# Queries with a third of the keys at whole width, the other keys in token halves, and new issue orders, in a windowed attention and MLP block

## The chip, the cores and the metric

One core of one Trainium2 chip runs the whole program. The metric is the device time of one execution in microseconds (us); less is better. Engines: PE is TensorE (matmuls; PEld its weight loads), DVE VectorE, ACT ScalarE, POOL GpSimd, SP SyncE, which here only issues DMAs.

## What is computed

The input is 32 images of 96 channels, 56 × 56 pixels. Each image is cut into 8 × 8 windows of 7 × 7 tokens:

```python
xn = layernorm(xw)                                  # per token, over 96 channels
q, k, v = split(xn @ qkv_w.T + qkv_b)               # 12 heads of 8
attn = softmax(q * SCALE @ k.T + bias[head])        # 49 x 49 per window and head
out = (attn @ v) @ proj_w.T + proj_b
x1 = x + out
bn = batchnorm(depthwise_conv3x3(x1))
y = bn + gelu(bn @ w1.T + b1) @ w2.T + b2           # hidden width 384
```

## The kernel before

A chunk is one row of windows of one image: 8 windows, 392 tokens. There are 256 chunks. Each engine has one list of steps; in step `s` (loops at L427, L557, L654, L825 and L234) it works on about ten chunks at once, each at another stage, so that chunk `c` needs some eight steps from load to output. The lists are written out by hand, in the order in which each engine issues its work; semaphores join them. `wait` waits for the producer, `free` for the last reader of a PSUM bank that is to be written again.

**The stages.** `centred` (L348) subtracts the mean with an fp32 matmul from `x_sb` into bank `d_ps`; ACT squares it, `variance` (L357) averages the squares into `b_ps`, `log_variance` and `root` (L535, L542) make 1/sqrt, DVE's `input_normal` (L804) makes `xn`, ACT's `input_high` (L549) its fp16 part `xh`, POOL's `input_low` (L594) the rest `xl`. Products of fp32 accuracy are made of three fp16 ones: high × high, high × low, low × high (`halves_three`, `whole_three`).

**Queries and keys.** `queries` (L365) writes 128 columns of weights (96 of queries and 32 that nobody reads) times 392 tokens into `a_ps`, `keys` (L372) the same for keys into `b_ps`. Both do so in two halves of 64 output partitions, three pairs of matmuls each. ACT's `query_high` and `key_high` (L511, L502) make fp16 `qh` and `kh`, 96 × 392, and DVE's `query_low` and `key_low` (L767) `ql` and `kl`. SP then copies these within SBUF into `q_all` and `k_all`, whose partitions are 32 rows of terms (4 terms × 8 dimensions) under the rows of bias, and whose free side has 12 heads × 8 windows × 50. Six DMAs per chunk do that (`term`, L209; 96 rows of 800 bytes each), and `max_scores` 0 waits for all six (L307).

**Scores.** `max_scores` p (L303) and `exp_scores` p (L282), p = 0 to 3 for two windows each, are 24 matmuls of 49 × 49, two windows side by side in the two halves of the array. DVE's `maxima` (L733) reduces the first; `maxima_rows` (L324) transposes the maxima, DVE's `maxima_out` copies them, and SP writes them as a row of `q_all` (`maximum_row`, L221), for which `exp_scores` 0 waits. ACT's `exp` (L468) makes the probabilities. `values` (L379) and `values_out` make `v32`; `values_times_p` p (L332) has 12 fp32 matmuls in four quarters of the array, each recorded as two passes. ACT's `outputs` writes them out, POOL's `to_channels` (L629) moves them with four DMAs, `log_sums`, `inverses` and `normalise` divide.

**The rest.** `projection` (L391) in fp32, `image_sum`, nine taps of the convolution (POOL two and a sum, DVE seven, L757), `image_high` and `image_low` on POOL, `hidden` k (L404), `gelu` k on ACT (L519), `second` k (L418, fp32, halves), and `block_out` (L795) on DVE, one per chunk. `hidden` 0, 1, 2 use `d_ps`, `a_ps`, `b_ps`; the three `second` accumulate in `d_ps`. ACT loads its function table twice per step (L559, L573).

**The order on PE** in a step before: `exp_scores` 2, `max_scores` 3, `projection`, `hidden` 0, `maxima_rows`, `hidden` 1, 2, `exp_scores` 3, `max_scores` 0, `second` 0, 1, 2, `keys`, `max_scores` 1, `queries`, `exp_scores` 0, `centred`, `max_scores` 2, `exp_scores` 1, `values_times_p` 2, 3, `variance`, `values`, `values_times_p` 0, 1.

Of the kernel before, what the change touches and what calls it, by code (L numbers as in the profile page):

```python
# [11 lines left out]
HD = C // HEADS  # L12
# [4 lines left out]
TOK = WS * WS  # L17
# [9 lines left out]
TERMS = 4 * HD  # L27
HIGH = ((2 * TERMS, 0, TOK),)
# [5 lines left out]
STEPS = CHUNKS + 11  # L34
# [4 lines left out]
def block_program(nc, x, w_qkv, b_qkv_row, b_v, w_proj, w_proj_rows, b_proj, ln_g, ln_b, bias_q,  # L39
                  conv_w, bn_g, bn_b, bn_mean, bn_var, w1, b1, w2, b2, eye, low, half, out):  # L40
    ctx = ExitStack()
    with ctx:
# [30 lines left out]
        qh, ql, kh, kl = (sb(n, [C, 2, NW * KP], F16) for n in ("qh", "ql", "kh", "kl"))  # L73
# [107 lines left out]
        def _(sp):  # L181
# [27 lines left out]
            def term(t, n, part, done, c):  # L209
                if not real(c):  # L210
                    return
                wait(sp, done, c)
                sp.dma_start(t[n:TERMS:4, c % 4, :, :], part[:, c % 2, :]).then_inc(exp_in[c % 4], 16)

            def first_term(t, n, part, done, c):
                if real(c):
                    wait(sp, sm_done[3], c - 4)
                    wait(sp, st_done[3], c - 4)
                    term(t, n, part, done, c)
# [29 lines left out]
        def _(pe):  # L249
# [8 lines left out]
            def halves_three(o, sh, sl, mh, ml):  # L258
# [3 lines left out]
                return halves(o, sl, mh, start=False)  # L262

# [68 lines left out]
            def values_times_p(c, p):  # L332
                if not real(c):
                    return
                if p == 0:
                    wait(pe, v32_done, c)
                wait(pe, p_done[p], c)
                if p == 0:
# [9 lines left out]
            def centred(c):  # L348
# [4 lines left out]
                free(pe, (y_done, c-8), (g_done[0], c-8), (xn_done, c-1))  # L353
# [3 lines left out]
            def variance(c):  # L357
# [4 lines left out]
                free(pe, (kl_done, c-1), (g_done[2], c-8), (sum_done, c-6), (lnv_done, c-1))  # L362
                mm(b_ps[0:C, 0:CT], avg[:, 0:C], sq[:, :], start=True, stop=True).then_inc(var_done, 1)  # L363

            def queries(c):  # L365
# [3 lines left out]
                free(pe, (g_done[1], c-7), (v32_done, c-2), (ql_done, c-1))  # L369
                halves_three(a_ps[0:128, 0:CT], wq_h[:, 0:128], wq_l[:, 0:128], xh[:, c % 2, :, 0:TOK], xl[:, c % 2, :, 0:TOK]).then_inc(q_done, 1)  # L370

            def keys(c):  # L372
# [3 lines left out]
                free(pe, (g_done[2], c-7), (sum_done, c-5), (lnv_done, c), (kl_done, c-1))  # L376
# [520 lines left out]
```

## Time and profile before

| | |
|---|---|
| median of 3 runs | 3174.46 us (3173.98 to 3175.64) |
| the profiled execution | 3164.1 us, its span 3162.3 us |
| busy: PE, PEld | 3029.4 us (96%), 2105.9 us (67%) |
| busy: DVE, ACT, POOL | 2888.8 (91%), 2768.5 (88%), 1956.6 us (62%) |
| DMA | 269,922 packets, 288.31 MB, mean 91 GB/s |
| granted PE clock, mean | 0.993 |

The span runs from the first to the last instruction. A matmul's record starts when it starts; its end is modelled, so consecutive records overlap and a busy share overstates how full PE is. "Idle before" counts the time in which the engine had no record open, and names what released it; "issue" means nothing that the profile shows. SPq is SP's issuing of DMAs.

### The profile page before, as it was taken

Reading aid. Unit: us, or ns where it says so; the run is one execution under the profiler, and the core shown is the slowest. Engines: PE = TensorE matmul, PEld = TensorE weight load, DVE = VectorE, ACT = ScalarE, POOL = GpSimd, SP = SyncE. Lnnn points to the kernel's source line nnn. Section 1 sums busy time; section 2 is a strip of 40 time slices with the busy share of each in tenths; the row PEclk is TensorE's granted clock in tenths of the full one; section 3 lists DMA queues with packets and bytes.
Section 4 is the critical chain, followed back from the end, with each engine's and each line's share of the span. In section 5 each row is a group of like instructions: output and inputs, shape, how many; then the busy total and the mean of one; then the engine's idle time right before and its main releaser. Section 6 shows DMA issues by size and latency. Waiting matters only on the chain.

```text
span 3162.3 us, 199772 instructions
## 1 busy us (share of the span) xinstructions
PE 3029.4 (96%) x88076; PEld 2105.9 (67%) x88076; DVE 2888.8 (91%) x4908; ACT 2768.5 (88%) x4867; POOL 1956.6 (62%) x2574
## 2 busy tenths in 40 slices
PE   3899999999999999999999999999999999999997
PEld 2666666666766666666666666666666676666663
DVE  4799999999999999999999999999999999999996
ACT  2799999989989999998989999988989999998986
POOL 2566666666666666666666666666666666666664
PEclk9999999999999999999999999999999999999998
DMA  1233333333333333333333333333333333333331
GB/s 40 86 91 96 91 96 94 92 95 91 97 91 94 95 94 95 96 91 95 91 96 94 94 96 94 92 96 91 95 95 93 96 97 93 95 98 91 95 92 41
DMA packets 269922, 288.31 MB, mean 91 GB/s; under 512 B 55651, under 2 KB 252580, under 8 KB 269062
## 3 DMA queue, kind: packets, MB, share of 16 engines
q1 hardware_dynamic: 236294, 198.40, 22.6%
q0 software_dynamic: 32768, 77.14, 7.0%
q8 instruction: 700, 11.47, 1.5%
q14 instruction: 160, 1.31, 0.1%
HBM read 39.34 MB, written 38.54 MB: 25 GB/s over the span
## 4 chain that ended last, share of the span: by engine, by line
PE 91%; issue 3%; ACT 2%; SPq 1%; DMA 1%; DVE 1%; POOL 0%; POOLq 0%; ACTq 0%; DVEq 0%
PE d_ps L255 21%; PE st_ps L299 12%; PE o_ps L345 11%; PE sm_ps L320 10%; PE b_ps L363 7%; PE b_ps L399 6%; PE a_ps L255 4%; PE b_ps L255 4%; PE a_ps L266 3%; PE a_ps L268 3%; PE a_ps L267 3%; PE d_ps L266 1%; PE d_ps L268 1%; PE b_ps L267 1%; PE d_ps L267 1%
## 5 line engine op out<-in xcount | busy, mean ns | idle before, releaser
L764 DVE SCALAR_TENSOR_TENSOR s<-ximg,cols,s 96x392 f32<-96x392 f32 x1792 | 1137.0, 635 | 30.7 <-POOL s L627 3.2
L738 DVE TENSOR_REDUCE mx<-sm_ps 128x12 f16<-128x588 f32 x1024 | 785.0, 767 | 127.7 <-PE sm_ps L320 125.1
L474 ACT ACTIVATE p<-st_ps 128x588 f32<-128x588 f32 x1024 | 672.4, 657 | 179.2 <-PE st_ps L299 176.1
L637 POOL DMA_DIRECT2D ox<-o_sb x1024 | 582.7, 572 | 30.8 <-ACT o_sb L499 17.2
L320 PEld LDWEIGHTS sm_ps<-k_all,q_all 127*49 127x49 f16 x24576 | 460.6, 104 | 171.5 <-issue 76.0
L255 PE MATMUL d_ps<-g,w_s 128*64 128x392 f32 x3072 | 560.2, 500 | 0.0
L299 PEld LDWEIGHTS st_ps<-q_all,k_all 128*49 128x49 f16 x24576 | 435.5, 103 | 157.2 <-issue 107.8
L610 POOL TENSOR_TENSOR s<-ximg,cols 96x392 f32<-96x392 f32 x256 | 216.0, 844 | 520.5 <-DVE y L801 519.9
L299 PE MATMUL st_ps<-q_all,k_all 128*49 128x49 f16 x24576 | 516.1, 186 | 21.4 <-issue 19.3
L320 PE MATMUL sm_ps<-k_all,q_all 127*49 127x49 f16 x24576 | 508.6, 186 | 25.9 <-issue 15.6
L599 POOL TENSOR_TENSOR xl<-xn,xh 96x392 f16<-96x392 f32 x256 | 258.8, 1011 | 273.6 <-ACT xh L555 256.5
L645 POOL CAST sh<-s 96x392 f16<-96x392 f32 x256 | 199.5, 779 | 350.0 <-DVE s L764 350.0
L345 PE MATMUL o_ps<-p,v 128*32 128x49 f32 x24576 | 384.9, 209 | 15.2 <-issue 13.1
L345 PEld LDWEIGHTS o_ps<-p,v 128*32 128x32 f32 x24576 | 308.9, 110 | 48.8 <-issue 18.8
L560 ACT ACT_TABLE_LOAD x256 | 328.4, 1283 | 4.5
L574 ACT ACT_TABLE_LOAD x256 | 328.4, 1283 | 4.4
L255 PEld LDWEIGHTS d_ps<-g,w_s 128*64 128x64 f32 x3072 | 197.2, 137 | 197.0 <-ACT g L525 116.0
L791 DVE TENSOR_TENSOR v<-a_ps,half_c 128x768 f32<-128x768 f32 x256 | 245.1, 958 | 36.1 <-PE a_ps L268 16.2
L627 POOL TENSOR_TENSOR s<-s,part 96x392 f32<-96x392 f32 x256 | 261.2, 1020 | 0.1
L652 POOL TENSOR_TENSOR sl<-s,sh 96x392 f16<-96x392 f32 x256 | 239.8, 937 | 20.5
L255 PE MATMUL d_ps<-x_sb,center 96*64 96x392 f32 x1024 | 224.1, 516 | 20.9 <-DMA x_sb<-in_x 20.9
L399 PE MATMUL b_ps<-ox,wp 96*96 96x196 f32 x1024 | 233.3, 350 | 6.3 <-DVE ox L755 5.6
(122 smaller groups left out, 5959.7 us busy)
## 6 DMA issues: line engine op xcount, KB each, us to landing
ox<-o_sb POOLq DMA_DIRECT2D x1024, 73.5 KB
k_all<-kh SPq DMA_DIRECT2D x512, 75.0 KB
q_all<-qh SPq DMA_DIRECT2D x512, 75.0 KB
x_sb<-in_x SPq DMA_DIRECT2D x256, 147.0 KB, 2.4
out<-y SPq DMA_DIRECT2D x256, 147.0 KB, 2.7
q_all<-ql SPq DMA_DIRECT2D x256, 75.0 KB
k_all<-kl SPq DMA_DIRECT2D x256, 75.0 KB
q_all<-mxt SPq DMA_DIRECT2D x256, 9.4 KB, 2.1
```

Source lines behind the costliest of these rows:

```text
L255: last = mm(o[64 * h:64 * h + 64], w[:, 64 * h:64 * h + 64], m, start=start, stop=stop)
L299: last = mm(st_ps[64 * w:64 * w + TOK, h // HH, c0:c0 + TOK], k_all[:, r, h, n:n + TOK], q_all[:, r, h, n:n + TOK], start=True, stop=True)
L320: last = mm(sm_ps[64 * w:64 * w + TOK, h // HH, c0:c0 + TOK], q_all[0:MAXROW, r, h, n:n + TOK], k_all[0:MAXROW, r, h, n:n + TOK], start=Tr ...
L345: last = mm(o_ps[32 * c4:32 * c4 + 32, at:at + TOK], v32[:, c % 2, h, p, :], p32[:, p, h, :], start=True, stop=True)
L399: last = mm(o, wp[:, 0:C], ox[:, c % 2, w, :].rearrange("c (n r k) -> c n r k", n=NP, k=WS), start=True, stop=True)
L474: af(p32[:, p, :, :].rearrange("p (b h) n -> p b h n", b=2), st_ps[:, :, 0:HALF].rearrange("p b (h n) -> p b h n", n=TOK), ACT.Exp).then_i ...
L560: act.preload_act_table_set("natural_log_exp_and_others")
L574: act.preload_act_table_set("gelu_and_others")
L627: tt(acc, acc, image(part[:, :]), ALU.add).then_inc(tap_done[1], 1)
L637: nc.gpsimd.dma_start(ox[:, c % 2, x4, :], o_sb[x4::4, c % 2, :, :]).then_inc(o_in[c % 2], 16)
L738: v.tensor_reduce(mx[:, c % 2, 0:HEADS, p].rearrange("p (b h) -> p b h", b=2), sm_ps[:, :, 0:HALF].rearrange("p b (h n) -> p b h n", n=TOK ...
L764: v.scalar_tensor_tensor(acc, image_rows(c, k // 3, k % 3), cw_c[:, k:k + 1], acc, ALU.mult, ALU.add)\
```

## The change

- `queries` writes its 96 rows and 32 rows of keys (four heads of each dimension, `K_WITH_Q`) at whole width, in three matmuls. `keys` makes the other 64 rows, into the same bank `a_ps`, for windows 0 to 3 in partitions 0 to 63 and windows 4 to 7 in partitions 64 to 127, in three pairs of 196 columns. `kh` and `kl` are now 128 × 196. The host orders the key columns to suit.
- The copies into `q_all` and `k_all` are twelve DMAs per chunk: three of queries (96 rows of 800 bytes), three of the third of the keys (32 rows of 800 bytes), six of the rest (64 rows of 400 bytes).
- The banks of `hidden` 0, 1, 2 become `a_ps`, `b_ps`, `d_ps`; `second` accumulates in `b_ps`, in the order 0, 2, 1.
- All five lists have a new order, with some work in the next or the previous step; there is one more step.

```diff
-STEPS = CHUNKS + 11
+K_WITH_Q = 4
+ARRIVALS = 12
+STEPS = CHUNKS + 12
-        qh, ql, kh, kl = (sb(n, [C, 2, NW * KP], F16) for n in ("qh", "ql", "kh", "kl"))
+        qh, ql = (sb(n, [128, 2, NW * KP], F16) for n in ("qh", "ql"))
+        kh, kl = (sb(n, [128, 2, NP * KP], F16) for n in ("kh", "kl"))
...
+            def third_of_keys(n, part, done, c):
...
+                wait(sp, done, c)
+                sp.dma_start(k_all[n:TERMS:4, c % 4, 0:K_WITH_Q, :], part[C:128, c % 2, :]).then_inc(exp_in[c % 4], 16)
+
+            def rest_of_keys(n, part, done, c):
...
+                wait(sp, done, c)
+                for i in range(2):
+                    sp.dma_start(k_all[n:TERMS:4, c % 4, K_WITH_Q:, i * NP * KP:(i + 1) * NP * KP],
+                                 part[64 * i:64 * i + 64, c % 2, :]).then_inc(exp_in[c % 4], 16)
...
             for s in range(STEPS):
+                store(s - 12)
                 load(s)
-                first_term(k_all, 0, kh, kh_done, s - 3)
-                term(k_all, 2, kh, kh_done, s - 3)
-                term(q_all, 0, qh, qh_done, s - 3)
-                term(q_all, 2, ql, ql_done, s - 3)
-                term(k_all, 1, kl, kl_done, s - 3)
-                term(q_all, 1, qh, qh_done, s - 3)
-                store(s - 11)
-                maximum_row(s - 4)
+                maximum_row(s - 5)
+                claim_terms(s - 3)
+                query_term(0, qh, qh_done, s - 3)
+                third_of_keys(2, qh, qh_done, s - 3)
+                third_of_keys(1, ql, ql_done, s - 3)
+                query_term(1, qh, qh_done, s - 3)
+                third_of_keys(0, qh, qh_done, s - 3)
+                query_term(2, ql, ql_done, s - 3)
+                rest_of_keys(0, kh, kh_done, s - 3)
+                rest_of_keys(2, kh, kh_done, s - 3)
+                rest_of_keys(1, kl, kl_done, s - 3)
...
+            def token_halves_three(o, sh, sl, mh, ml):
+
+                terms = ((sh, mh), (sh, ml), (sl, mh))
+                for i, (s, m) in enumerate(terms):
+                    for h in range(2):
+                        last = mm(o[64 * h:64 * h + 64], s, m[:, NP * h:NP * h + NP], start=i == 0, stop=i == 2)
+                return last
...
-                    wait_ring(pe, exp_in, c, 6 * 16)
+                    wait_ring(pe, exp_in, c, ARRIVALS * 16)
...
             def queries(c):
                 if not real(c):
                     return
                 wait(pe, xl_done, c)
-                free(pe, (g_done[1], c-7), (v32_done, c-2), (ql_done, c-1))
-                halves_three(a_ps[0:128, 0:CT], wq_h[:, 0:128], wq_l[:, 0:128], xh[:, c % 2, :, 0:TOK], xl[:, c % 2, :, 0:TOK]).then_inc(q_done, 1)
+                free(pe, (g_done[0], c-7), (v32_done, c-2), (kl_done, c-1), (ql_done, c-1))
+                whole_three(a_ps[:, 0:CT], wq_h[:, 0:128], wq_l[:, 0:128], xh[:, c % 2, :, 0:TOK], xl[:, c % 2, :, 0:TOK]).then_inc(q_done, 1)
 
             def keys(c):
                 if not real(c):
                     return
                 wait(pe, xl_done, c)
-                free(pe, (g_done[2], c-7), (sum_done, c-5), (lnv_done, c), (kl_done, c-1))
-                halves_three(b_ps[0:128, 0:CT], wq_h[:, 96:224], wq_l[:, 96:224], xh[:, c % 2, :, 0:TOK], xl[:, c % 2, :, 0:TOK]).then_inc(k_done, 1)
+                free(pe, (ql_done, c), (g_done[0], c-7), (v32_done, c-2), (kl_done, c-1))
+                token_halves_three(a_ps[:, 0:NP * TOK], wq_h[:, 128:192], wq_l[:, 128:192], xh[:, c % 2, :, 0:TOK], xl[:, c % 2, :, 0:TOK]).then_inc(k_done, 1)
...
-            hidden_ps = {0: d_ps, 1: a_ps, 2: b_ps}
+            hidden_ps = {0: a_ps, 1: b_ps, 2: d_ps}
...
                 if k == 0:
-                    free(pe, (xn_done, c+7), (y_done, c-1), (g_done[0], c-1))
+                    free(pe, (v32_done, c+5), (kl_done, c+6), (ql_done, c+6), (g_done[0], c-1))
...
+                    free(pe, (g_done[1], c), (sum_done, c+2), (lnv_done, c+7), (y_done, c-1))
+                halves(b_ps[0:128, 0:CT], w2_s[:, k, :], g[:, k, :], start=k == 0, stop=k == 1).then_inc(s_done[k], 1)
...
             for s in range(STEPS):
+                keys(s - 1)
+                second(s - 8, 2)
+                second(s - 8, 1)
+                exp_scores(s - 3, 0)
+                max_scores(s - 2, 1)
+                centred(s)
+                exp_scores(s - 3, 1)
+                max_scores(s - 2, 2)
+                values_times_p(s - 4, 3)
+                variance(s)
+                values(s - 2)
+                exp_scores(s - 3, 2)
+                projection(s - 5)
+                max_scores(s - 2, 3)
+                values_times_p(s - 3, 1)
+                values_times_p(s - 3, 0)
+                hidden(s - 7, 0)
+                hidden(s - 7, 2)
+                hidden(s - 7, 1)
+                maxima_rows(s - 2)
+                queries(s)
+                values_times_p(s - 3, 2)
+                exp_scores(s - 3, 3)
+                second(s - 7, 0)
+                max_scores(s - 1, 0)
...
             for s in range(STEPS):
+                if real(s - 8):
+                    act.preload_act_table_set("gelu_and_others")
+                gelu(s - 8, 0)
+                outputs(s - 4, 0)
+                gelu(s - 8, 1)
+                query_high(s - 1)
                 gelu(s - 8, 2)
                 if real(s - 8):
                     act.preload_act_table_set("natural_log_exp_and_others")
                 exp(s - 4, 3)
                 key_high(s - 1)
-                query_high(s - 1)
                 exp(s - 3, 0)
                 log_sums(s - 5)
                 square(s)
...
                 log_variance(s)
                 root(s)
                 exp(s - 3, 2)
-                if real(s - 7):
-                    act.preload_act_table_set("gelu_and_others")
-                gelu(s - 7, 0)
-                outputs(s - 3, 0)
                 input_high(s)
-                gelu(s - 7, 1)
...
             for s in range(STEPS):
-                first_product(s - 6)
-                second_product(s - 6)
-                image_high(s - 7)
-                image_low(s - 7)
                 add_products(s - 6)
+                input_low(s)
                 to_channels(s - 4)
-                input_low(s)
+                second_product(s - 5)
+                first_product(s - 5)
+                image_high(s - 6)
+                image_low(s - 6)
...
             for s in range(STEPS):
+                maxima_out(s - 3)
+                tap(s - 7, 4)
+                query_low(s - 1)
+                tap(s - 7, 5)
+                maxima(s - 2, 0)
+                tap(s - 7, 6)
+                key_low(s - 1)
+                block_out(s - 8)
+                maxima(s - 2, 1)
+                tap(s - 7, 7)
+                tap(s - 7, 8)
+                normalise(s - 5)
                 maxima(s - 2, 2)
+                input_normal(s)
                 values_out(s - 2)
-                input_normal(s)
+                image_sum(s - 5)
                 maxima(s - 2, 3)
-                image_sum(s - 5)
                 tap(s - 6, 2)
-                maxima_out(s - 2)
                 tap(s - 6, 3)
-                tap(s - 6, 4)
-                maxima(s - 1, 0)
-                tap(s - 6, 5)
-                tap(s - 6, 6)
-                block_out(s - 7)
-                maxima(s - 1, 1)
-                key_low(s)
-                query_low(s)
-                tap(s - 6, 7)
-                tap(s - 6, 8)
-                normalise(s - 4)
```

PE's order in a step is shown above as it stands after the change. In `key_high` and `key_low` the operands become `a_ps[:, 0:NP * TOK]` and the 128 × 196 tiles; the waits of ACT and POOL on `hid_done`, `s_done` and `pv_done` follow the new orders.

## Rows read from the trace of the kernel before

**Rows 1.** The page, part 1: busy time, share of the span, instructions.
```profile
PE 3029.4 (96%) x88076; PEld 2105.9 (67%) x88076; DVE 2888.8 (91%) x4908; ACT 2768.5 (88%) x4867; POOL 1956.6 (62%) x2574
```

**Rows 2.** The instructions of line 801, `block_out`: ns min/median/max, first and last start.
```profile
L801 DVE SCALAR_TENSOR_TENSOR y<-d_ps,cols,s x256: 611/622/623, 126.0 to 3159.3; 96x392 f32<-96x392 f32 x128
```

**Rows 3.** Timeline of PE in one turn: start us, duration us, line, operands, count.
```profile
1501.51 2.17 PE L255 MATMUL d_ps<-g,w_s 128*64 128x392 f32 x12
...
1503.52 0.34 PE L255 MATMUL b_ps<-xh,wq_h 97*64 97x392 f16 x2
...
1504.36 0.34 PE L255 MATMUL a_ps<-xh,wq_h 97*64 97x392 f16 x2
...
1504.87 0.49 PE L299 MATMUL st_ps<-q_all,k_all 128*49 128x49 f16 x24
...
1505.88 0.49 PE L320 MATMUL sm_ps<-k_all,q_all 127*49 127x49 f16 x24
...
1506.20 0.48 PE L299 MATMUL st_ps<-q_all,k_all 128*49 128x49 f16 x24
...
1506.62 0.72 PE L345 MATMUL o_ps<-p,v 128*32 128x49 f32 x47
...
1507.66 0.23 PE L345 MATMUL o_ps<-p,v 128*32 128x49 f32 x1 [0.33 <-issue]
...
1507.83 0.90 PE L363 MATMUL b_ps<-sq,avg 96*96 96x392 f32 x2
...
1509.16 0.73 PE L345 MATMUL o_ps<-p,v 128*32 128x49 f32 x48
...
1509.82 0.50 PE L299 MATMUL st_ps<-q_all,k_all 128*49 128x49 f16 x24
...
1510.58 0.90 PE L399 MATMUL b_ps<-ox,wp 96*96 96x196 f32 x4
...
1511.32 0.33 PE L266 MATMUL d_ps<-sh,w_h 96*128 96x392 f16 x1
...
1511.48 0.33 PE L267 MATMUL d_ps<-sl,w_h 96*128 96x392 f16 x1
```

**Rows 4.** PE's waits over the span: total us, times, longest us.
```profile
PE st_ps L299 <- issue: 19.3, 44, 0.8
...
PE sm_ps L320 <- issue: 15.6, 31, 1.7
PE o_ps L345 <- issue: 13.1, 30, 1.5
```

**Rows 5.** The page, part 3, the instruction queue: packets, MB, share of 16 engines.
```profile
q8 instruction: 700, 11.47, 1.5%
```

**Rows 6.** Timeline of ACT and DVE around the layer norm and the table load.
```profile
1508.76 0.58 ACT L540 ACTIVATE sq<-b_ps,cols 96x392 f32<-96x392 f32 x1 [0.41 <-PE b_ps L363]
...
1509.38 0.53 ACT L547 ACTIVATE sq<-sq 96x392 f32<-96x392 f32 x1
...
1510.15 0.56 DVE L810 TENSOR_TENSOR xn<-d_ps,sq 96x392 f32<-96x392 f32 x1
...
1511.05 1.28 ACT L574 ACT_TABLE_LOAD   x1
...
1512.34 0.59 ACT L525 ACTIVATE g<-d_ps,b_c 128x392 f32<-128x392 f32 x1
...
1513.12 0.53 ACT L555 ACTIVATE xh<-xn 96x392 f16<-96x392 f32 x1
```

**Rows 7.** The page, part 5, `maxima`: busy us, mean ns, idle before.
```profile
L738 DVE TENSOR_REDUCE mx<-sm_ps 128x12 f16<-128x588 f32 x1024 | 785.0, 767 | 127.7 <-PE sm_ps L320 125.1
```

**Rows 8.** SP's issues: a term (timeline), the maximum row (ns), and its landing (page).
```profile
1508.82 0.67 SPq L213 DMA_DIRECT2D q_all<-qh  x1
...
L225 SPq DMA_DIRECT2D q_all<-mxt x256: 547/563/581, 66.7 to 3105.1; - x128
...
q_all<-mxt SPq DMA_DIRECT2D x256, 9.4 KB, 2.1
```

More of the change, by code:

```diff
@@ L207, in load, with claim_terms, query_term @@
                 sp.dma_start(x_sb[:, at:at + CT], dram_rows(x, c)).then_inc(x_in[c % 8], 16)
-            def term(t, n, part, done, c):
+            def claim_terms(c):
+                if not real(c):
+                    return
+                wait(sp, sm_done[3], c - 4)
+                wait(sp, st_done[3], c - 4)
+            def query_term(n, part, done, c):
                 if not real(c):
@@ L212, in term @@
                 wait(sp, done, c)
[L213 to L219, printed above, removed]
+                sp.dma_start(q_all[n:TERMS:4, c % 4, :, :], part[0:C, c % 2, :]).then_inc(exp_in[c % 4], 16)
+            def third_of_keys(n, part, done, c):
+                if not real(c):
+                    return
+                wait(sp, done, c)
+                sp.dma_start(k_all[n:TERMS:4, c % 4, 0:K_WITH_Q, :], part[C:128, c % 2, :]).then_inc(exp_in[c % 4], 16)
+            def rest_of_keys(n, part, done, c):
+                if not real(c):
+                    return
+                wait(sp, done, c)
+                for i in range(2):
+                    sp.dma_start(k_all[n:TERMS:4, c % 4, K_WITH_Q:, i * NP * KP:(i + 1) * NP * KP],
+                                 part[64 * i:64 * i + 64, c % 2, :]).then_inc(exp_in[c % 4], 16)
             def maximum_row(c):
@@ L352, in centred @@
                 wait_ring(pe, x_in, c)
-                free(pe, (y_done, c-8), (g_done[0], c-8), (xn_done, c-1))
+                free(pe, (g_done[2], c-8), (xn_done, c-1))
                 at = c % CPI * CT
@@ L423, in second @@
                 if k == 0:
-                    free(pe, (g_done[0], c), (xn_done, c+7), (y_done, c-1))
-                halves(d_ps[0:128, 0:CT], w2_s[:, k, :], g[:, k, :], start=k == 0, stop=k == 2).then_inc(s_done[k], 1)
+                    free(pe, (g_done[1], c), (sum_done, c+2), (lnv_done, c+7), (y_done, c-1))
+                halves(b_ps[0:128, 0:CT], w2_s[:, k, :], g[:, k, :], start=k == 0, stop=k == 1).then_inc(s_done[k], 1)
             for s in range(STEPS):
-                exp_scores(s - 4, 2)
-                max_scores(s - 3, 3)
-                projection(s - 6)
-                hidden(s - 8, 0)
-                maxima_rows(s - 3)
-                hidden(s - 8, 1)
-                hidden(s - 8, 2)
-                exp_scores(s - 4, 3)
-                max_scores(s - 2, 0)
-                second(s - 8, 0)
+                keys(s - 1)
+                second(s - 8, 2)
                 second(s - 8, 1)
-                second(s - 8, 2)
-                keys(s - 1)
+                exp_scores(s - 3, 0)
                 max_scores(s - 2, 1)
-                queries(s - 1)
-                exp_scores(s - 3, 0)
                 centred(s)
+                exp_scores(s - 3, 1)
                 max_scores(s - 2, 2)
-                exp_scores(s - 3, 1)
-                values_times_p(s - 4, 2)
                 values_times_p(s - 4, 3)
@@ L495, in outputs @@
                     return
-                wait(act, pv_done[1 if half == 0 else 3], c)
+                wait(act, pv_done[0 if half == 0 else 3], c)
                 if half == 0:
@@ L765, in tap, with low_part @@
                  .then_inc(tap_done[k], 1)
[L767 removed]
+            def low_part(c, ps, n, hi, dst, done, out_):
                 if not real(c):
@@ L859 @@
     order = np.arange(C).reshape(HEADS, HD).T.reshape(-1)
-    perm = np.concatenate([order, C + order, 2 * C + np.arange(C)])
+    by_dim = np.arange(C).reshape(HEADS, HD).T
+    keys = np.concatenate([by_dim[:, 0:K_WITH_Q].reshape(-1), by_dim[:, K_WITH_Q:].reshape(-1)])
+    perm = np.concatenate([order, C + keys, 2 * C + np.arange(C)])
     at = np.stack(np.meshgrid(np.arange(WS), np.arange(WS), indexing="ij"), -1).reshape(-1, 2)
```

36 lines of the change are left out of this document (17 added, 19 removed).

## The prediction

> **What bounds the kernel now.** I read the busy shares first: TensorE (PE) 96% of the span, VectorE 91%, ScalarE 88% [rows 1]. A busy share of pipelined matmuls proves little, so I measured one turn. `block_out` starts 256 times, from 126.0 to 3159.3 us: (3159.3 − 126.0) / 255 = 11.895 us per chunk [rows 2]. Then I took the start of each PE block and of the one after it [rows 3]. Per chunk: the three `second` 2.01, `queries` 0.51 (1504.36 to 1504.87) and `keys`, of the same shapes, as much, `exp_scores` 0 with `centred` 1.01, a scores block 0.32 (1505.88 to 1506.20), 0.42 where another tile shape follows (1506.20 to 1506.62; also in the pair `exp_scores` 2 and `max_scores` 3, 0.76 from 1509.82 to 1510.58), two `values_times_p` 0.66 (1509.16 to 1509.82), `variance` and `values` 1.33, projection 0.74, and the nine hidden matmuls with the transpose 9 × 0.165 + 0.15 = 1.64. In the order of the program that is 2.01 + 0.51 + 0.33 + 0.51 + 1.01 + 0.32 + 0.42 + 0.66 + 1.33 + 0.66 + 0.34 + 0.42 + 0.74 + 1.64 + 0.34 + 0.32 = 11.56 us. So 0.335 us of a turn is not PE work, 85 us over the run.
>
> What is it? Waits of PE for another engine's semaphore are few; the list of waits names "issue", no releaser, for 48.0 us in 105 stalls [rows 4]. The stalls lie inside blocks, where no semaphore stands: at 1507.66 the last matmul of a `values_times_p` pair is late, and the pair takes 1.21 instead of 0.66 us [rows 3]. A modelled matmul of 0.19 to 0.21 us hides some 0.18 us of each stall, so they are worth about 48 + 105 × 0.18 = 67 us, most of the 85. The instruction queue moved 11.47 MB in 700 pieces [rows 5], 2.7 pieces of 16 KB per chunk. PE alone executes 2 × 88,076 instructions [rows 1], 252 per piece. I read the stalls as PE having run through a piece before the next is there. They come late in the dense stretch, when few columns stand behind each instruction: from `exp_scores` 0 (1504.87) to the end of `max_scores` 3 (1510.58) PE runs some 470 of a chunk's 700 instructions in 5.2 us of work.
>
> **The change on PE.** `keys` keeps six matmuls, each with 196 columns instead of 392; two column halves run side by side, as each scores block and each pair now shows (0.51 us is three pairs of 392 columns at 0.17). Three pairs of 196 columns cost 3 × (0.082 + 0.007) = 0.27, so −0.24 us. The bounds are −0.26 (half) and 0 (if halves with different moving data did not overlap; but the scores blocks have different data in both halves and do 24 matmuls in 0.32 us). `queries` becomes three whole matmuls at the hidden matmuls' 0.165: 0.495, −0.02 us. Together −0.26.
>
> The order costs something back. Each change of tile width costs about 0.09 us: 0.42 against 0.32 for the same block, and projection 0.74 against 0.66, two fp32 passes of 392 columns at 2.01 / 6 (there it is a change of type) [rows 3]. `second` and `centred` followed by an fp16 block cost 0.04 (1.01 − 0.32 = 0.69 for the two passes of `centred`). The old order has eight changes at 0.09 and two at 0.04. The new one has ten (before and after `values_times_p` 3, after `variance`, after `values`, before and after projection, before `values_times_p` 1, before `hidden` 0, before and after `values_times_p` 2) and three at 0.04: +0.22 us. The bounds are 0 and, if the unseen projection-to-scores change costs twice as much, +0.31. PE's work is then 11.56 − 0.26 + 0.22 = 11.52 us. The edit that gives the change its name is all but paid back by its order.
>
> The Trainium skill (TensorEngine Tiling (Array Packing), Key Properties) speaks against the order: "Mode switching requires drain", a change of mode and not of tile. By that rule the count would go from six to nine, with +0.27 in place of +0.22. The trace agrees for width and shows 0.09 for a change of type as well.
>
> **The stalls.** I summed block times over every run of 256 instructions round the turn. Before, a run that starts anywhere from `keys` to the middle of `values_times_p` 3, a third of all, lasts 2.5 to 3.2 us; the densest is `exp_scores` 0 to `values_times_p` 3, 248 instructions in 2.4 us. In the new order `second` 1 and 2, projection and the hidden matmuls stand between the scores blocks; there is one run as dense, but only 2% of the starts are under 3.2 us and the middle one is 3.8. The stalls should fall from 0.33 to about 0.03 us a turn; bounds 0 and 0.33 (nothing changes, the first rival). I take 0.03, because the stalls follow density.
>
> The Trainium skill (Runtime: NRT & Kernel Launch, Instruction fetch mechanics) states blocks of 16 KB, as [rows 5] shows, but that the fetch is hidden behind dispatch. By that rule the stalls are not the fetch and need not go. The trace speaks against it: 105 stalls without a releaser.
>
> **New waits.** I laid the new lists of all engines against PE's new times (`keys` at 0). `variance` starts at 4.06, `log_variance` 0.93 later, `root` 0.62 after that and 0.53 long, `input_normal` 0.56, `input_high` 0.53, the table load 1.28, `gelu` 0 0.59 [rows 6], with about 0.05 at four hand-overs: `a_ps` is free for `queries` 5.25 us after `variance` starts. PE gets there after 5.13. So PE waits 0.10 to 0.12; the wait of `hidden` 0 for `values_out` (0.06) lies inside it. `max_scores` 2 starts 1.34 us after `max_scores` 1, and the reduction (started 0.53 after its block, 0.77 long [rows 7], hand-over 0.08) needs 1.38: 0.04. In all 0.15; bounds 0 and 0.4. `exp_scores` 0 and 1 and `values_times_p` 3 keep 0.04 to 0.2 us of slack.
>
> **What is hidden.** ScalarE's `key_high` and VectorE's `key_low` halve (about −0.15 and −0.2 us); neither engine is the bound, and what it gives is the slack just used. ScalarE's list still sums to about 10.4 and VectorE's to 10.5 us. `input_low`, `image_low` and the output DMAs on POOL keep over 1 us. SP issues twelve transfers instead of six. A term takes 0.67 us and the small maximum row 0.56 [rows 8]; thirds and halves should lie between, and I take 0.72, a term with the step to the next. Twelve take 8.6; with store, load and maximum row at 0.6 each, 10.4 of 11.7 us. They begin when `query_high` ends (10.5), the last is issued near 18.9 and lands 2.1 us later [rows 8], at 21.0; `max_scores` 0 wants it at 22.7. The maximum row is issued at 10.2 and lands at 12.3; `exp_scores` 0 wants it at 13.2. Without that slack each late 0.1 us would be PE's. The extra step at the end and about 0.6 us more latency are nothing.
>
> **Sum.** 11.52 + 0.03 + 0.15 = 11.70, against 11.895: −0.195 × 255 = −50 us. From the profiled execution's own 3164.1 us that is 3114; the median of the runs shown is 10.4 us above it, so 3124. I say 3122, since part of the new waits gives the fetch time to catch up.
>
> **Rivals.** (1) The stalls stay: 11.52 + 0.33, plus 0.05 of waits that they don't cover, is 11.90 and leaves 3174, within 0.2% or just about it. For it: the densest run is as dense as before. Against it: they come at the end of a long dense stretch, which is broken up. Chance 0.15. (2) Slower: the closed chain from `variance` over the table load and `gelu` 0 to `queries` takes the lead. Now a table load follows `input_high` at once, and nothing on PE can pass `queries`. It decides from 0.31 us above PE's 5.13 on: 11.52 + 0.03 + 0.04 + 0.31 = 11.90. If `log_variance`, `root` and `input_normal` each come 0.1 us late (ScalarE or VectorE has to finish something else first), it is 0.12 + 0.3 = 0.42, the turn 12.01 and the time 3174 + 0.115 × 255 = 3204; at 0.2 us each 3280. For it: no slack stands in the chain. Against it: both engines come to it idle in my layout. Chance 0.13. (3) SP becomes the bound: from (11.7 − 1.8) / 12 = 0.82 us per issue on. At 0.9 the turn is 12.6 and the time 3355. No issue in [rows 8] is that long. Chance 0.04. (4) The halves of `keys` do not overlap: 3122 + 0.24 × 255 = 3183. Chance 0.03. (5) All waits vanish: 11.52 gives 3078. Chance 0.15. My forecast has 0.50.
>
> **Numbers.** About 0.2% is what can be told from no change here. Faster by more: 0.50 + 0.15 and half of rival 1: 0.72; same 0.08; slower 0.20. The range goes from rival 5 to a little beyond rival 4, 3075 to 3190: it leaves out most of rivals 2 and 3.
>
> **What would show it.** PE's "issue" idle in the scores and `values_times_p` blocks falls from 48 us to under 10. `keys` lasts 0.27 us and `queries` 0.5 to 0.6, PE waits for `gelu` at `queries` some 0.1 us each turn, `block_out` comes every 11.7 us, and no wait for a term's DMA appears. Wrong if the issue stalls stay, if PE waits longer for ScalarE or VectorE than 0.3 us a turn, or if SP is never idle.

## The result and the profile after

The changed kernel takes 3354.4 us (3353.5 to 3357.4, 4 runs), the kernel before 3174.2 in the same session: ratio 1.0564, 95% interval 1.0547 to 1.058. It is 180 us slower; I had forecast 52 us less.

The page of the changed kernel, part 1, answers to [rows 1]. VectorE (DVE) is busy 154 us longer for the same 4908 instructions, although its `key_low` got shorter:

```profile
PE 3108.5 (93%) x87308; PEld 2120.5 (63%) x87308; DVE 3043.3 (91%) x4908; ACT 2784.4 (83%) x4867; POOL 1939.3 (58%) x2574
```

The instructions of `block_out`, now line 830, answer to [rows 2]:

```profile
L830 DVE SCALAR_TENSOR_TENSOR y<-b_ps,cols,s x256: 606/622/624, 130.4 to 3349.1; 96x392 f32<-96x392 f32 x128
```

(3349.1 − 130.4) / 255 = 12.62 us a turn, against 11.895: 0.727 × 255 = 185 us, all of the difference. The median turn is 12.51 and half of the turns lie between 12.49 and 12.76, so nearly every turn is long.

PE's waits over the span answer to [rows 4]:

```profile
PE a_ps L290 <- DVE ql L801: 135.3, 243, 1.3
...
PE o_ps L374 <- issue: 13.7, 32, 1.1
...
PE sm_ps L349 <- issue: 7.0, 14, 1.1
...
PE st_ps L328 <- DMA q_all<-mxt: 6.1, 11, 1.6
```

The same view for the weight loads:

```profile
PEld a_ps L290 <- issue: 155.3, 247, 2.0
...
PEld st_ps L328 <- DMA q_all<-mxt: 50.9, 121, 1.8
```

The "issue" stalls of the score and probability blocks fell from 48 us in 105 to 21 in 46. In their place stands one wait in nearly every turn: `keys` (L290) waits for VectorE's `query_low` of the same chunk (L801), since both now use bank `a_ps`. The weight loads of `keys` stand idle in the same stretch (0.64 us from 1516.96 in the turn below, while PE's own gap is 0.56), so their 155.3 us are the same wait over again, not a further one. PE's timeline shows it, with the blocks that [rows 3] priced:

```profile
1514.56 0.33 PE L295 MATMUL a_ps<-xh,wq_h 97*128 97x392 f16 x1
...
1515.16 0.47 PE L374 MATMUL o_ps<-p,v 128*32 128x49 f32 x24
...
1516.58 0.49 PE L349 MATMUL sm_ps<-k_all,q_all 127*49 127x49 f16 x24
1517.63 0.28 PE L290 MATMUL a_ps<-xh,wq_h 97*64 97x196 f16 x2 [0.56 <-DVE ql L801]
...
1517.89 1.51 PE L276 MATMUL b_ps<-g,w_s 128*64 128x392 f32 x8
1519.26 0.50 PE L328 MATMUL st_ps<-q_all,k_all 128*49 128x49 f16 x24
...
1521.79 0.90 PE L392 MATMUL b_ps<-sq,avg 96*96 96x392 f32 x2
...
1523.56 0.90 PE L428 MATMUL b_ps<-ox,wp 96*96 96x196 f32 x4
1524.39 0.50 PE L349 MATMUL sm_ps<-k_all,q_all 127*49 127x49 f16 x24
```

`max_scores` 0 (L349, 1516.58) is done after 0.3 us, `keys` starts 1.05 us after it began: PE stands for about 0.7 us. Why is `query_low` late? VectorE's timeline:

```profile
1513.93 1.86 DVE L793 SCALAR_TENSOR_TENSOR s<-ximg,cols,s 96x392 f32<-96x392 f32 x2
1515.72 0.19 DVE L777 COPY mxt<-sm_ps 48x100 f16<-48x100 f16 x1
1515.84 1.17 DVE L793 SCALAR_TENSOR_TENSOR s<-ximg,cols,s 96x392 f32<-96x392 f32 x1
1516.93 0.55 DVE L801 SCALAR_TENSOR_TENSOR ql<-a_ps,qh 128x392 f16<-128x392 f32 x1
1517.40 0.61 DVE L793 SCALAR_TENSOR_TENSOR s<-ximg,cols,s 96x392 f32<-96x392 f32 x1
...
1523.90 0.56 DVE L839 TENSOR_TENSOR xn<-d_ps,sq 96x392 f32<-96x392 f32 x1 [0.62 <-ACT sq L576]
...
1526.46 1.86 DVE L793 SCALAR_TENSOR_TENSOR s<-ximg,cols,s 96x392 f32<-96x392 f32 x2
```

and POOL's for the same stretch:

```profile
1513.44 2.27 POOL L666 DMA_DIRECT2D ox<-o_sb  x4
1515.72 0.85 POOL L647 TENSOR_TENSOR part<-ximg,cols 96x392 f32<-96x392 f32 x1
```

A tap takes 0.61 us (1517.40). Tap 4, beside POOL's `second_product` (L647), takes 1.17; of the pair of taps 2 and 3 (1.86 for both) the first ends after 0.61, tap 3 takes 1.21 and ends when the four DMA issues, behind which the product is queued, end. Tap 3 takes over 0.9 us in 92% of the turns, tap 4 in 97%. In the kernel before, POOL's two products ran beside other work in most turns (its tap 4, the slowest, takes over 0.9 us in 10%); its timeline of the two engines:

```profile
1504.51 0.84 POOL L610 TENSOR_TENSOR s<-ximg,cols 96x392 f32<-96x392 f32 x1 [1.85 <-DVE y L801]
1505.31 0.84 POOL L618 TENSOR_TENSOR part<-ximg,cols 96x392 f32<-96x392 f32 x1
```

```profile
1504.56 0.77 DVE L738 TENSOR_REDUCE mx<-sm_ps 128x12 f16<-128x588 f32 x1 [0.20 <-PE sm_ps L320]
1505.25 0.56 DVE L772 SCALAR_TENSOR_TENSOR kl<-b_ps,kh 96x392 f16<-96x392 f32 x1
1505.72 0.55 DVE L772 SCALAR_TENSOR_TENSOR ql<-a_ps,qh 96x392 f16<-96x392 f32 x1
```

Those VectorE instructions read PSUM, and none is longer there than elsewhere. A tap reads two operands (`ximg` and the running sum `s`) from SBUF. Such a case the Trainium skill names (SBUF — State Buffer, Who interferes with whom): a VectorE instruction with two SBUF inputs contends with a GpSimd instruction that reads SBUF, the port pair that they share is an exclusive lock, and the order of issue decides which of the two blocks. The trace agrees in size: tap 4 is 0.56 us longer, most of the 0.85 us of the product. It also shows the other order: POOL's cast `sh` starts 0.14 us (median) after VectorE's product of `ox` and `inv`, both in SBUF; there it is the cast that is long, 0.78 us in the median and 0.51 at least, while VectorE's instruction keeps its 0.56.

**Theory A, the loop of `query_low`.** From one `query_low` to the next in these timelines: to `keys` 0.70 (1517.63 − 1516.93), to `variance` 4.16, to `log_variance` 0.93, to `root` 0.62, to `input_normal` 0.56 (1523.90), to tap 2 2.56 (1526.46), to `query_low` 3.00 (1516.93 − 1513.93). The sum is 12.53, the median turn being 12.51. It is closed: each step starts when the last ends. Without the 1.16 us that taps 3 and 4 lose, it would be 11.37 and below PE's own work.

**Theory B, the maximum row.** The row's DMA lands a median 2.7 us after its issue (2.1 before), and `exp_scores` 0 waits for it in 121 turns. **Theory C:** the new operand layout, not the order, costs the time; twelve transfers are too many. **Theory D:** both loops are nearly as long, so that taking away one shows little.

### The profile page after: what moved, and what is told of

It reads as the page before. It is cut to its first block, busy times and chain, and to the rows that moved or that the text cites. A ratio compares the mean times of both kernels' runs of the same rounds, so it can differ in the third digit from the quotient of the medians.

```text
span 3352.1 us, 199772 instructions
## 1 busy us (share of the span) xinstructions
PE 3108.5 (93%) x87308; PEld 2120.5 (63%) x87308; DVE 3043.3 (91%) x4908; ACT 2784.4 (83%) x4867; POOL 1939.3 (58%) x2574
## 3 DMA queue, kind: packets, MB, share of 16 engines
q8 instruction: 694, 11.37, 1.5%
## 4 chain that ended last, share of the span: by engine, by line
PE 41%; DVE 34%; issue 14%; ACT 9%; DMA 2%; SPq 0%; POOL 0%; POOLq 0%; DVEq 0%; ACTq 0%
DVE s L793 12%; PE b_ps L276 10%; DVE v L820 7%; PE b_ps L392 6%; PE sm_ps L349 6%; PE d_ps L276 5%; PE st_ps L328 5%; DVE mx L767 5%; ACT sq L569 4%; ACT sq L576 4%; DVE ximg L849 4%; PE o_ps L374 4%; DVE ql L801 3%; PE a_ps L290 3%; DMA q_all<-mxt 2%
## 5 line engine op out<-in xcount | busy, mean ns | idle before, releaser
L793 DVE SCALAR_TENSOR_TENSOR s<-ximg,cols,s 96x392 f32<-96x392 f32 x1792 | 1408.9, 786 | 21.6 <-POOL s L656 2.8
L276 PE MATMUL b_ps<-g,w_s 128*64 128x392 f32 x3072 | 613.3, 502 | 4.0 <-ACT g L554 3.1
L328 PEld LDWEIGHTS st_ps<-q_all,k_all 128*49 128x49 f16 x24576 | 455.7, 103 | 254.9 <-ACT p L503 108.3
L349 PEld LDWEIGHTS sm_ps<-k_all,q_all 127*49 127x49 f16 x24576 | 438.2, 103 | 181.6 <-issue 176.8
L349 PE MATMUL sm_ps<-k_all,q_all 127*49 127x49 f16 x24576 | 515.4, 186 | 8.3 <-issue 7.0
L374 PE MATMUL o_ps<-p,v 128*32 128x49 f32 x24576 | 439.2, 210 | 14.5 <-issue 13.7
L374 PEld LDWEIGHTS o_ps<-p,v 128*32 128x32 f32 x24576 | 327.8, 109 | 124.7 <-issue 104.7
L839 DVE TENSOR_TENSOR xn<-d_ps,sq 96x392 f32<-96x392 f32 x256 | 143.9, 562 | 197.5 <-ACT sq L576 197.5
L628 POOL TENSOR_TENSOR xl<-xn,xh 96x392 f16<-96x392 f32 x256 | 232.7, 909 | 147.7 <-ACT xh L584 129.8
L276 PEld LDWEIGHTS b_ps<-g,w_s 128*64 128x64 f32 x3072 | 202.3, 137 | 97.6 <-issue 94.5
```

The costliest lines, as they stand in the source:

```text
L276: last = mm(o[64 * h:64 * h + 64], w[:, 64 * h:64 * h + 64], m, start=start, stop=stop)
L328: last = mm(st_ps[64 * w:64 * w + TOK, h // HH, c0:c0 + TOK], k_all[:, r, h, n:n + TOK], q_all[:, r, h, n:n + TOK], start=True, stop=True)
L349: last = mm(sm_ps[64 * w:64 * w + TOK, h // HH, c0:c0 + TOK], q_all[0:MAXROW, r, h, n:n + TOK], k_all[0:MAXROW, r, h, n:n + TOK], start=Tr ...
L374: last = mm(o_ps[32 * c4:32 * c4 + 32, at:at + TOK], v32[:, c % 2, h, p, :], p32[:, p, h, :], start=True, stop=True)
L793: v.scalar_tensor_tensor(acc, image_rows(c, k // 3, k % 3), cw_c[:, k:k + 1], acc, ALU.mult, ALU.add)\
```

## The experiments

Each is the changed kernel with one edit, except where said. Ratios are to the kernel before on the same chip.

**Second product left out** (e1):

```diff
                 to_channels(s - 4)
-                second_product(s - 5)
                 first_product(s - 5)
```

> The changed kernel without POOL's second_product (the second tap's product is left out; the sum reads zeros). Theory A, that POOL's tensor_tensor on the image holds something that VectorE's taps with two SBUF operands need: taps 3 and 4 fall from about 1.2 to 0.61 us each, query_low ends in time, the turn falls from 12.62 to 11.7 us, about 3120 us. Rival B, that tap 3 is slowed by POOL's four DMA issues and only tap 4 by the product: tap 3 stays 1.2, turn about 12.1, about 3230 us. Rival C, that the twelve SP issues or late terms set the turn: it stays above 12.4, 3300 us or more.

3328.9 us, ratio 1.0425 (1.0386 to 1.0464). The wait for the product is left out with it. Only 0.14 us of the turn went (12.48 mean), so theory A's 3120 us was missed and the time is the one that I had given to rival C, though the waits are not its waits. Taps 3 and 4 were back at 0.62, and PE waited for `query_low` in seven turns in place of 243. It waited for another thing; PE's and PEld's waits and the page, part 5:

```profile
PE a_ps L290 <- DVE ql L799: 3.9, 7, 1.3
...
PE st_ps L328 <- DMA q_all<-mxt: 48.1, 100, 2.1
PE o_ps L374 <- issue: 46.9, 51, 1.5
```

```profile
PEld st_ps L328 <- DMA q_all<-mxt: 158.0, 179, 2.3
```

```profile
L791 DVE SCALAR_TENSOR_TENSOR s<-ximg,cols,s 96x392 f32<-96x392 f32 x1792 | 1131.1, 631 | 21.9 <-POOL s L655 3.2
```

A mean tap of 631 ns, against 786 in the changed kernel. So the product does lengthen the taps, the wait for `query_low` does come from that, and it was not the only thing that held the turn.

**Second product elsewhere** (e2: ahead of `to_channels`; e3: behind `first_product`):

```diff
-                to_channels(s - 4)
                 second_product(s - 5)
+                to_channels(s - 4)
```
```diff
-                second_product(s - 5)
                 first_product(s - 5)
+                second_product(s - 5)
```

> The changed kernel with second_product moved ahead of to_channels, so that it starts while VectorE reduces maxima 3 from PSUM. Theory A: taps 3 and 4 are 0.61 us, tap 2 is held for up to 0.4 us, the turn is 11.8 to 12.0 us, 3140 to 3190. Rival B (the DMA issues hold the taps): taps 3 and 4 stay slow, as they still lie beside to_channels; turn 12.4 or more, above 3290.

> The changed kernel with second_product behind first_product, as in the kernel before. Theory A: taps 3 and 4 are 0.61 us, taps 7 and 8 lie beside the two products and one of them takes up to 1.2 us; that delays normalise and the sums, which have some slack; turn 11.8 to 12.1, 3140 to 3210 us. Rival B: tap 3 stays 1.2, turn above 12.3.

e2: 3367.2, ratio 1.0545 (1.0508 to 1.0583). e3: 3335.0, ratio 1.0435 (1.0392 to 1.0478). Wherever the product goes, the taps beside it pay: tap 2 at 0.78 us in e2 (3 and 4 at 0.62), tap 7 at 0.81 and mostly tap 8 at 1.08 in e3. PE's wait for the row stood in both (PEld: 175.8 us in e2, 160.3 in e3), and its landing took a median 3.2 us. Both missed theory A's 3140 to 3210 us as e1 did. In e2 `to_channels` with its four DMAs goes out behind the product, and nothing was gained.

**The layout alone, in the order of before** (e4: the kernel before with the new key columns and tiles and the twelve transfers; `keys` stays in `b_ps`, so that the wait for `query_low` isn't there). Its core against the kernel before:

```diff
-                first_term(k_all, 0, kh, kh_done, s - 3)
-                term(k_all, 2, kh, kh_done, s - 3)
...
+                claim_terms(s - 3)
+                rest_of_keys(0, kh, kh_done, s - 3)
+                rest_of_keys(2, kh, kh_done, s - 3)
+                query_term(0, qh, qh_done, s - 3)
+                third_of_keys(2, qh, qh_done, s - 3)
+                third_of_keys(0, qh, qh_done, s - 3)
+                query_term(1, qh, qh_done, s - 3)
+                rest_of_keys(1, kl, kl_done, s - 3)
+                third_of_keys(1, ql, ql_done, s - 3)
+                query_term(2, ql, ql_done, s - 3)
```

> The kernel before with only the new layout: whole-width queries with a third of the keys, token-half keys (in b_ps), twelve term transfers; all orders of before. Theory A: PE saves 0.26 us in the two blocks and pays 0.18 for two more changes of tile width, no tap is slow; the fetch stalls stay; turn about 11.8, 3150 us. Rival C (twelve issues or late terms): slower than before, above 3190.

3803.4, ratio 1.1881 (1.1843 to 1.1919): on rival C's side (above 3190), and far from theory A's 3150. And the control for it (e12): the kernel before, where each of its six terms is copied in two DMAs of four windows:

```diff
-                sp.dma_start(t[n:TERMS:4, c % 4, :, :], part[:, c % 2, :]).then_inc(exp_in[c % 4], 16)
+                for i in range(2):
+                    a, b = i * NP * KP, (i + 1) * NP * KP
+                    sp.dma_start(t[n:TERMS:4, c % 4, :, a:b], part[:, c % 2, a:b]).then_inc(exp_in[c % 4], 16)
```

> The kernel before, its layout and all orders, with each of the six term transfers cut into two halves of the windows (twelve issues of 37.5 KB, the same bytes). If twelve issues in SP's queue are what made e4 slow, this one has the loop keys, key_high, twelve issues, landing, max_scores 0, second, keys as well: turn 14 us or more, ratio 1.15 to 1.2. If e4 was slow for its new columns or banks, this one stays below 1.03.

3904.7, ratio 1.2277 (1.2248 to 1.2306), above the 1.15 to 1.2 that I had expected; so with the old columns and banks, and nothing new but the number of transfers, the kernel is as slow. PE's waits, in e4 and in e12:

```profile
PE sm_ps L349 <- DMA q_all<-ql: 509.8, 253, 6.1
```

```profile
PE sm_ps L322 <- DMA q_all<-qh: 561.5, 256, 6.3
```

and SP's timeline in e4:

```profile
1526.36 2.62 SPq L235 DMA_DIRECT2D k_all<-kh  x4
1529.03 0.71 SPq L222 DMA_DIRECT2D q_all<-qh  x1
1529.78 0.70 SPq L228 DMA_DIRECT2D k_all<-qh  x1
```

An issue of 25 KB costs SP 0.6 to 0.7 us, as one of 75 KB does [rows 8]. Twelve take 7.7 us from the first issue to the last one's start, where six took 3.6, and in the old order they lie in a loop: `keys`, `key_high`, twelve issues, landing, `max_scores` 0, the three `second`, `keys`. So the change needs its order: what theory C blames is real, but in the changed kernel its place is not on PE's path. There a term is waited for in four turns at most, 2.0 us in all, and SP idles for the maxima:

```profile
SPq L242 <- DVE mxt L777: 486.4, 255, 10.2
```

**Both causes taken away.** An unchanged copy (c_after) as a control; e5 without the maximum row's DMA and the waits for it (`exp` has a factor of 0.25, so that nothing overflows); e6 with the edits of e5 and e1 together:

```diff
                 wait(sp, mxt_out, c)
-                sp.dma_start(q_all[MAXROW:MAXROW + 1, c % 4, :, :].rearrange("p h (n c) -> p (h n) c", c=2 * KP),
-                             mxt[:, c % 2, :, :].rearrange("m w t -> m (w t)")).then_inc(row_in[c % 2], 16)
...
-                if p == 0:
-                    wait_ring(pe, row_in, c)
...
-                wait_ring(dve, row_in, c - 2)
```

> The changed kernel itself, as the yardstick of this chip: 1.055 to 1.06 of the kernel before; the maximum row lands 2.7 us after its issue at the median, taps 3 and 4 take 1.2 us.

> The changed kernel without the copy of the maximum row (left out: the DMA of the maxima and exp_scores' wait for it; the exponent is scaled by 0.25 so that nothing overflows). Theory of two loops: the loop over second_product, taps 3 and 4, query_low and keys stands alone at about 12.5 us; little gain, ratio to before 1.04 to 1.055. If the row alone is the bound, the ratio falls to 1.0 or below.

> Without second_product and without the maximum row's copy (both left out). Theory of two loops: both are gone and PE is the bound again, turn 11.7 us, ratio 0.98 to 0.99; the sum of what each alone gives is much less than this. If there is a third loop, for instance the twelve issues on SP, the ratio stays above 1.02.

The control: 3359.4, ratio 1.0556 (1.0527 to 1.0584). e5: 3318.0, 1.0429 (1.0402 to 1.0456). e6: 3156.9, 0.9924 (0.9902 to 0.9946). e5 gives 1.3 points of the ratio, e1 1.4 (against the 1.0564 of its own kernel; e1 ran on another chip than the control), both together 6.3. That is theory D: two loops side by side, either of which holds the turn near 12.5. With both gone the turn is 11.84 (median 11.77), and PE is the bound again. PE's waits in e6 hold next to nothing, and of two matmuls of one scores or probability block 49 start over 120 ns apart, where before had 141:

```profile
PE a_ps L288 <- DVE ql L794: 3.7, 6, 1.3
```

e5 and e6 do less work than the changed kernel. What the two loops cost with all work kept, the repairs below show.

The second loop, in e1's own trace (means of the middle 235 turns): from PE's `maxima_rows` to VectorE's copy 0.60 us, to SP's issue 0.23, to `exp_scores` 0 3.47 (nearly all of it the landing), and from there to the next `maxima_rows` 8.21. They sum to 12.51, the mean turn. The last piece is 7.76 in the median (7.73 in the changed kernel's turn above, 1519.26 to 1526.99); in its mean it holds the stalls that PE has within blocks, for which this loop has no slack.

**The repairs, with all work kept.** e7 was to hold the product until tap 6 of an earlier chunk and to send the row earlier; on VectorE the copy goes one tap ahead, on PE `maxima_rows` ahead of `hidden` 1:

```diff
-                hidden(s - 7, 1)
                 maxima_rows(s - 2)
+                hidden(s - 7, 1)
...
                 wait(pool, tap_done[1], c - 1)
+                wait(pool, tap_done[6], c - 2)
...
-                maxima_out(s - 3)
                 tap(s - 7, 4)
...
                 tap(s - 6, 2)
+                maxima_out(s - 2)
                 tap(s - 6, 3)
```

> The changed kernel with two mends: second_product waits for tap 6 of two chunks earlier, so that it runs beside key_low, block_out and maxima 1, which read PSUM; and the maxima are transposed before hidden 1 and copied between taps 2 and 3, so that the row is issued some 0.6 us earlier. Theory of two loops: no tap above 0.8 us, PE waits for the row under 0.2 us a turn, turn 11.7 to 11.9, ratio 0.98 to 1.0. If it stays above 1.03 the theory lacks a loop.

3352.4, ratio 1.0541 (1.0514 to 1.0568). My wait named chunk c − 2, whose tap 6 was long done: the product stayed where it was, and the taps stayed at 786 ns. So the 0.98 to 1.0 that I expected was missed for want of the edit. Only the row was repaired, which makes e7 the test of that alone. PE's and PEld's waits in e7:

```profile
PE a_ps L290 <- DVE ql L802: 111.9, 242, 1.3
```

```profile
PEld st_ps L328 <- DMA q_all<-mxt: 10.9, 24, 1.4
```

The wait for the row fell from 50.9 to 10.9 us and the time did not move: loop A alone holds the turn. With the wait on tap 6 of chunk c − 1 (e11 alone, e10 with the row's edit):

> The changed kernel with only that wait of second_product. Theory of two loops: the taps are at 0.61 us, but the loop over the maximum row is then alone, as in e1: PE waits 0.5 us or more a turn for the row's DMA, ratio 1.03 to 1.045. If the ratio is at e10's, the row was no loop.

> As e7, but second_product waits for tap 6 of the chunk before its own; in e7 the wait was for one chunk earlier still, long past when the product came up, so the product stayed on taps 3 and 4. Nothing is left out. Theory of two loops: taps 3 and 4 take 0.61 us, the row costs PE under 0.2 us a turn, turn 11.7 to 11.9, ratio to the kernel before 0.985 to 1.0. Rival, a third loop: above 1.02.

e11: 3302.1, ratio 1.0353 (1.0314 to 1.0391). e10: 3249.5, ratio 1.0214 (1.019 to 1.0237), and of its taps only tap 7 is at 0.78. The waits for the row in e11 and in e10:

```profile
PEld st_ps L328 <- DMA q_all<-mxt: 143.1, 168, 2.1
```

```profile
PEld st_ps L328 <- DMA q_all<-mxt: 52.3, 75, 2.2
```

VectorE's timeline in e10:

```profile
1528.86 1.28 DVE L794 SCALAR_TENSOR_TENSOR s<-ximg,cols,s 96x392 f32<-96x392 f32 x2
1530.23 0.57 DVE L802 SCALAR_TENSOR_TENSOR ql<-a_ps,qh 128x392 f16<-128x392 f32 x1
```

With all work kept, the row's repair alone gives 0.15 points of the ratio (e7), the product's alone 2.0 (e11), both 3.4 (e10): the row counts once loop A is repaired, as theory D has it. But e10 missed its 0.985 to 1.0; it lies at the 1.02 that I had set for a third loop and does not beat the kernel before. e10's median turn, 11.89, lies beside that of before (11.82); the mean is 12.21, since 29 of 250 turns take over 13 us, where before has 9. Besides the row, its waits hold "issue" stalls of nearly a microsecond:

```profile
PE o_ps L374 <- issue: 34.6, 38, 1.7
```

**The row ahead of store and load on SP** (e13, on e10):

```diff
-                store(s - 12)
-                load(s)
                 maximum_row(s - 5)
+                store(s - 12)
+                load(s)
```

> The version before it with both repairs (second_product behind tap 6, the maximum row two taps earlier; 3249 us, mean turn 12.21, median 11.89), with one edit: SP issues the maximum row ahead of store and load instead of behind them. There the load of x is issued right before the row, its issue takes up to 1.3 us where POOL issues its own four DMAs at that time, and the row lands a median 2.8 us after its issue (2.1 before the change). Theory (what is left over the kernel before is the row's loop): the row lands in about 2.1 to 2.4 us and is issued up to a microsecond earlier, PE's waits for it go, the mean turn falls to 11.9 to 12.0 and the time to 3170 to 3200, ratio 1.00 to 1.005. Rival (what is left is fetch stalls and the late VectorE list, the row being a follower): 3235 to 3260, ratio 1.017 to 1.025. Second rival: the terms, now behind store and load, come late for max_scores 0 and SP's waits for image_sum hold them: PE waits for a term's DMA appear and it is slower than 3260.

3305.6, ratio 1.0386 (1.0348 to 1.0424): worse than e10, where I expected 1.0 to 1.005. (The row's edit in it is one tap and one hidden block, not two taps.) The row did land sooner, median 2.35 us, and PE waited for it less (PEld 38.9 us in 63), so the row's loop is not what is left. A quarter of the turns are under 11.85, but 44 now take over 13. On PE a term was hardly waited for (PEld 11.2 us in 28 for `kl`, in e10 2.9), so the second rival's size came true without its mechanism. What grew are PE's "issue" stalls and a wait for the maxima:

```profile
PE o_ps L374 <- issue: 44.5, 38, 1.9
PE sm_ps L349 <- DVE mx L768: 25.6, 61, 0.9
```

These rare long turns can be placed. In e10 a turn that holds a stall of over 0.3 us within a block lasts 13.35 us in the mean (38 of 250 turns), the others 12.01, and 25 of the 29 turns over 13 us hold one; in e13 38 of the 44, in the kernel before all nine.

The stalls lie at fixed places of PE's program. Counted over its matmuls, weight loads and semaphore instructions, 55 of e10's 57 gaps over 60 ns within blocks stand a multiple of 256 instructions apart, to within three; so do 60 of e13's 61, 82 of e1's 84, and 122 of 125 in the kernel before. There PE runs 179,224 such instructions, 700 times 256 and 24 more, and the instruction queue moved 700 pieces [rows 5]. PE goes on 1.2 to 1.6 us after a piece's packet has ended. So I read these stalls as waits for the next piece of the program. Two things go with them. In the kernel before, the run of 256 ahead of a stall is short: 2.9 us in the median, 4.2 elsewhere. In e10 it is 3.8 against 4.4, but there the packet starts 2.5 us after PE has entered the run, elsewhere 1.0. Why it starts late is open, and so is what else makes e13 slower than e10.

## Why the prediction was wrong

- **The step that failed** is the paragraph "What is hidden": "VectorE's [list still sums] to 10.5 us" and "`input_low`, `image_low` and the output DMAs on POOL keep over 1 us". I summed each engine's list at the durations of the old trace and asked only for slack between them. Those durations belong to the neighbours they had: a mean tap of 635 ns beside POOL work that seldom touched it. The new POOL list puts `second_product` beside taps 3 and 4; its taps take 1409 us instead of 1137, 1.06 us a turn, and the page puts the mean tap at 786 ns. e1 and e6 show it. The turn was 12.62 in place of 11.70.
- **The wait I did not list.** Under "New waits" I had `queries` on `gelu` 0 and `max_scores` 2 on `maxima` 1. The diff also adds `(ql_done, c)` to `keys`: the joint bank makes PE wait for VectorE in the middle of a turn. That wait closed loop A. My slower rival 2 had such a loop from `variance`, but ran it over the table load and `gelu` 0. It went through `input_normal` and VectorE's list. Both errors were needed: with its taps at 0.61 loop A would be 11.37 us, below PE's work.
- **The maximum row.** "Issued at 10.2 and lands at 12.3; `exp_scores` 0 wants it at 13.2" left 0.9 us. It takes 2.7 us here, 3.2 in e2, e3 and e11, 3.3 in e1, and its copy stood behind the long tap 3. Of the 0.9 us, 0.6 to 1.2 went on the landing alone. e7 shows that PE's wait for it cost nothing by itself in the changed kernel, e1 and e6 that it takes over once loop A is repaired. e5's 1.3 points for the row's whole absence are more than e7's 0.15; its one trace is of an execution of 8481.6 us, in which the fp32 matmuls of `second` and `centred` take 1.3 us in place of 0.5, and can't tell; that difference stays open.
- **PE's work** was right block by block, but too low in sum. `keys` takes 0.26 us (1517.63 to 1517.89; forecast 0.27), `queries` 0.60 with the change of width behind it (1514.56 to 1515.16; 0.50 + 0.09). Projection with the step to `max_scores` 3 takes 0.83 (1523.56 to 1524.39), 0.09 above my value: the bound I had kept for that change. e6's turn of 11.84, with all waits gone, against my 11.52 + 0.03 and these 0.09 leaves 0.2 us that I had not seen. e6's trace has half of it: its blocks' medians sum to 11.76, with `exp_scores` 1 at 0.37 (I had 0.32), `maxima_rows` at 0.10 (0.06) and each lone `values_times_p` at 0.40 (0.37). The same sum for the kernel before is 11.56. So the new order makes PE's own work 0.2 us longer, where I had forecast 0.04 less, and even with both loops gone the gain was 0.8%.
- **The stalls** went the forecast way, not as far: starts over 120 ns apart within blocks fell from 141 to 66, and to 49 in e6; the "issue" waits from 48 to 21 us, not under 10. Part of the fall in the changed kernel is that PE waits elsewhere: in e1 the gaps within blocks sum to 74.5 us, more than the 50.1 before. The reading as waits for the next piece of the program is borne out by their places, 256 instructions apart, and the dense runs did go: of the runs of 256, 39% took under 3.5 us before and 4% do now. What I had at nothing is a stall where the piece itself comes late.
- **SP** was right, rival 3 wrong, although its 3355 us is the time measured: an issue takes 0.61 to 0.71 us, not 0.9, and SP has idle time in every turn. My test "or if SP is never idle" says so; the test "PE waits longer for ScalarE or VectorE than 0.3 us a turn" is the one that came true: 135.3 / 255 = 0.53 us for VectorE's `query_low` alone.
- **The range** left out a loss of more than 16 us, because "slower" was priced as a few late hand-overs. A closed loop with two doubled instructions in it cost 0.69 us in the median turn (12.51 against 11.82), some 175 us.

## What to carry to other kernels

A duration taken from a trace holds for its neighbours: when an order changes on two engines, list what will run beside each instruction, and where VectorE reads two operands from SBUF, keep POOL's elementwise work off that stretch. When a change puts two results into one bank, follow the new wait round to itself and add up the loop; slack counted along a list does not show it. If one repair gives little, look which other loop has taken over, and take both away before judging either. And when PE stalls without a releaser, count its instructions from one stall to the next.

## What the runs showed that I had not expected

- A tap of 0.61 us takes 1.17 to 1.21 us beside POOL's `second_product`; also where POOL is still issuing the DMAs ahead of the product (tap 3, 1513.93 in the timeline above). With the product left out and the same DMAs issued there (e1), the tap takes 0.62. Tap 7, in most turns beside `first_product`, takes 0.61 to 0.81 (medians of the changed kernel and the runs made from it), tap 2 in e2 0.78, so the loss depends on how the two meet.
- The 9.4 KB row of maxima lands 2.0 to 4.2 us after its issue (5% to 95% over these kernels): medians 2.1 before, 2.7 in the changed kernel, 3.2 to 3.3 in e1, e2, e3, where PE waits for it. What makes it long is not shown: the few rows that met no `ox` transfers landed in 2.0 to 2.1 us, but nearly all rows of the kernel before met them and took 2.1; with the load of x behind it and not ahead (e13) it fell from 2.7 to 2.4.
- Issuing a DMA of a third of the bytes (25 KB against 75 KB) costs SP the same 0.6 to 0.7 us. Six more issues per chunk, with nothing else changed, made the kernel before 23% slower (e12).
- PE's stalls within blocks come at one place in its runs of 256 instructions, for each of which the instruction queue moved one piece of 16 KB (700 of each before). They can be told from other waits by counting instructions. Breaking up the dense stretches did not end them: their sum is 50.1 us before, 43.6 in e10, 53.8 in e13 and 74.5 in e1, and only e6 has few (8.5).
